# Chunked delta-rule recurrence: decays made in the setup, norms from turned rows, system in wide products, roots on GpSimd, new engine orders

## What is computed

```
q = silu(conv4(x @ Wq)); k, v = silu(conv4(x @ Wk)), silu(conv4(x @ Wv))     # 1 q, 3 k, 3 v per token and head
beta = 2 * sigmoid(x @ Wb); g = -exp(A_log) * softplus(x @ Wa + dt_bias)
q, k = l2norm(q) * d**-0.5, l2norm(k)
per token:  S = S * exp(g)
            for i in 0..2:  S = S + beta_i * k_i (v_i - k_i' S)'
            o = q' S
y = rmsnorm(o) * rms_weight * silu(x @ Wg);  out = y @ Wo
```

## Time and profile before

| what | value |
|---|---|
| median of 3 runs | 4379.42 us |
| the profiled execution's own time | 4341.66 us |
| its span, first to last instruction | 4339.9 us |
| TensorE (PE) busy | 3964.4 us, 91% |
| VectorE (DVE) busy | 3489.6 us, 80% |
| ScalarE (ACT) busy | 3345.5 us, 77% |
| GpSimd (POOL) busy | 2389.8 us, 55% |
| mean granted TensorE clock | 0.966 of 2.4 GHz |
| setup ends, recurrence ends | about 100 us, about 3482 us |

### The profile page before, as it was taken

One profiled execution on the slowest core, in us unless ns is written; L12 is line 12 of the kernel. 1 busy time (PEld: TensorE's weight loads), 2 busy tenths in 40 slices (PEclk: granted clock), 3 DMA queues, 4 the chain that ended last, 5 costly groups with the idle time before them and its releaser, 6 DMA issues. The chain is left out here.

```text
span 4339.9 us, 131624 instructions
## 1 busy us (share of the span) xinstructions
PE 3964.4 (91%) x47876; PEld 3634.2 (84%) x47876; DVE 3489.6 (80%) x9822; ACT 3345.5 (77%) x9032; POOL 2389.8 (55%) x2511
## 2 busy tenths in 40 slices
PE   1999999999999999999999999999999885999991
PEld 0799888999988888999989899999999775888881
DVE  6899999999998888999989999999999734444446
ACT  3888888888888888888888888888888722556551
POOL 3566667666766666666766666766676414000005
PEclk6999999999999999999999999999999987999995
DMA  6222333323333333223323333323333154666664
GB/s 255 66 83 87 87 87 91 87 79 84 102 87 74 82 84 89 75 83 89 100 78 85 87 85 88 92 87 83 76 104 89 45 177 141 231 226 239 232 225 130
DMA packets 307824, 485.08 MB, mean 112 GB/s; under 512 B 38784, under 2 KB 252800, under 8 KB 288384
## 3 DMA queue, kind: packets, MB, share of 16 engines
q1 hardware_dynamic: 290448, 449.65, 35.2%
q0 software_dynamic: 6144, 16.79, 1.2%
q10 hardware_dynamic: 10608, 10.23, 0.7%
HBM read 352.02 MB, written 107.75 MB: 106 GB/s over the span
## 5 line engine op out<-in xcount | busy, mean ns | idle before, releaser
L1111 DVE SCALAR_TENSOR_TENSOR conv_acc<-bank,conv_sb,conv_acc 128x256 f32<-128x256 f32 x2304 | 1089.7, 478 | 14.1 <-ACT conv_acc L922 4.7
L671 PE MATMUL bank<-x_cur,w_cur 128*128 128x259 f16 (+1 forms) x6144 | 856.7, 276 | 27.9 <-DVE v_rows L1099 24.9
L1170 DVE CAST_PREDICATED xs_lev<-mask_sb,bank 128x256 f16<-128x256 uint16 x1536 | 663.2, 432 | 98.6 <-PE bank L735 75.3
L982 ACT ACTIVATE inv<-bank 128x256 f16<-128x256 f32 x1536 | 605.4, 394 | 74.3 <-PE bank L747 51.6
L671 PEld LDWEIGHTS bank<-x_cur,w_cur 128*128 128x128 f16 (+1 forms) x6144 | 565.0, 98 | 93.1 <-DVE v_rows L1099 25.8
L1293 POOL TENSOR_TENSOR decay<-decay_tok,cst 128x512 f32<-128x512 f32 x256 | 320.0, 1273 | 489.7 <-ACT decay_tok L956 489.7
L991 ACT ACTIVATE invt<-bank 128x256 f16<-128x256 f32 x1280 | 508.3, 397 | 88.4 <-PE bank L759 72.2
L790 PE MATMUL bank<-state,kq_t 128*128 128x128 f32 x2048 | 448.3, 301 | 2.0 <-DVE state L1193 2.0
L735 PE MATMUL bank<-inv,n_high 128*128 128x64 f16 x6144 | 432.9, 193 | 3.8 <-issue 1.5
L798 PE MATMUL bank<-rhs,inv_t 128*128 128x128 f32 x2048 | 428.7, 302 | 3.1 <-DVE rhs L1186 3.1
L805 PE MATMUL bank<-w_sol,k_rows 128*128 128x128 f32 x2048 | 422.1, 298 | 2.1 <-ACT w_sol L1001 1.9
(11 more groups left out here) (245 smaller groups left out, 11482.7 us busy)
## 6 DMA issues: line engine op xcount, KB each, us to landing
w_cur<-w_parts_scratch SPq DMA_DIRECT2D x128, 1024.0 KB, 10.5
ew<-e_parts_scratch SPq DMA_DIRECT2D x117, 896.0 KB, 6.2
x_cur<-x_parts_scratch SPq DMA_DIRECT2D x128, 259.0 KB, 7.2
x_slots<-no_rows SPq DMA_DIRECT2D x128, 256.0 KB, 10.4
e_parts_scratch<-e_pair SPq DMA_DIRECT2D x96, 224.0 KB, 7.4
o_rows<-w_sol SPq DMA_DIRECT2D x512, 32.0 KB, 4.1
y_scratch<-y_buf SPq DMA_DIRECT2D x128, 128.0 KB, 10.1
y_in<-y_scratch SPq DMA_DIRECT2D x32, 512.0 KB, 4.1
```

Source lines behind the costliest of these rows:

```text
L671: last = mm(bank[i % 2][:, 0:PW], w_cur[k.i % 2][:, wp, kt, c * P:(c + 1) * P].bitcast(BF16 if wp else F16), x_cur[k.i % 2][:, xp, kt, 0:P ...
L982: a(half(inv[k.i % R_LEV][g][:], l, 0), packed(halves(LEVT), l), ACT.Copy).then_inc(t_kept.sem, 1)
L1111: v.scalar_tensor_tensor(acc, bank[at % 2][:, i:i + TB], conv_sb[:, k.h, c, i:i + 1], acc, ALU.mult, ALU.add).then_inc(tap_step.sem if i < ...
L1170: v.copy_predicated(half(xs_lev[g][l - 1][:], l, 0), half(mask4(l), l, 0).bitcast(U16), packed(halves(LEVX), l)).then_inc(x_kept.sem, 1)
```

## The change

In the setup, the decays of all blocks are made at once: VectorE multiplies (spans), TensorE sums in f32 products of 128x512, two per stretch, ScalarE takes exp and stores 512 KB per stretch to DRAM (d_dram). In the recurrence they are loaded (load_decay) instead of computed. The key scale goes into them on GpSimd (key_decay), so that system is one 128x512 VectorE operation per group. Keys are copied unscaled to k_rows by ScalarE, which squares and sums the turned rows (square_rows); the scale of the keys moves to keep_w as a scale operand. The query's norm rides in a 129th column of w_sol and o_rows. Both roots are taken on GpSimd with the power operation. norms, norms_q, decays, exp_decay, key_ln, var_ln and var_root on ScalarE are gone, and with them the table loads. The GpSimd channel's taps become one product of four windows and two additions. y_buf is a ring of 3, w_sol of 4. All six lists have a new order; stages are counted to 23, and the work lies at k[18] to k[22]. The pieces below come, in this order, from: the sizes, the setup's ScalarE, its TensorE, SyncE (load_decay and list), ScalarE, VectorE and GpSimd (powers and list).

```diff
-R_SQ = 1
+R_Y = 3
+R_CK = 3
-R_W = 3
+R_W = 4
-STAGES = 8
+STAGES = 23
...
+                    for tb in range(NTB):
+                        if tb >= 2:
+                            act.wait_ge(d_stored[tb % 2], 16 * (tb // 2))
+                        for i in range(2):
+                            act.wait_ge(spans_summed, 2 * tb + i + 1)
+                            nc.scalar.activation(decay_out[tb % 2][:, 2 * i:2 * i + 2].rearrange("p a b -> p (a b)"), bank[6 + i][:],
+                                                 ACT.Exp).then_inc(decayed, 1)
+                        act.wait_ge(decayed, 2 * tb + 2)
+                        act.dma_start(d_dram[tb], decay_out[tb % 2][:]).then_inc(d_stored[tb % 2], 16)
...
+                    for tb in range(NTB):
+                        pe.wait_ge(spans_made, tb + 1)
+                        for i in range(2):
+                            if tb:
+                                pe.wait_ge(decayed, 2 * tb - 1 + i)
+                            nc.tensor.matmul(bank[6 + i][:], cst_once[:, C_LATER_OWN],
+                                             g_upto[tb % 2][:, 2 * i:2 * i + 2].rearrange("p a b c -> p (a b c)"),
+                                             start=True, stop=True).then_inc(spans_summed, 1)
...
+                    def load_decay(k):
...
+                        at_least(sp, key_decayed, k.n - 1)
+                        sp.dma_start(decay_in[k.i % 2][:].rearrange("p a b -> p (a b)"),
+                                     bass.AP(own.tensor, own.offset, [[0, 4]] + list(own.ap))).then_inc(decay_ld[k.i % 2], 16)
...
                     def body(k):
-                        move_outputs(k[5])
-                        load(k[0])
-                        store(k[7])
-                        pieces(k[4])
+                        pieces(k[0])
+                        load_decay(k[3])
+                        store(k[9])
+                        load(k[3])
+                        move_outputs(k[7])
...
+                    def keep_k(g, k):
+                        done(act, rows_made, ("keys", g), k.n)
+                        a(k_rows[k.i % R_ROWS][:, 4 * g:4 * g + 4].rearrange("p a b -> p (a b)"), ROWS[:], ACT.Copy).then_inc(keys_kept.sem, 1)
+
+                    def square_rows(u, k):
+                        done(act, keys_kept, u // 4, k.n)
+                        a(square_out[:, u], k_rows[k.i % R_ROWS][:, u], ACT.Square, accum_out=sums[k.i % 2][:, u:u + 1])\
+                            .then_inc(squared.sem, 1)
+
+                    def keep_q(k):
+                        act.wait_ge(normed, k.n + 1)
+                        a(w_sol[k.i % R_W][96:128, :, P], k_sq[k.i % 2][96:128, :], ACT.Copy).then_inc(q_kept, 1)
...
-                        a(w_sol[k.i % R_W][:, c], chain(k), ACT.Copy).then_inc(sol_kept.sem, 1)
+                        a(w_sol[k.i % R_W][:, c, 0:P], chain(k), ACT.Copy, scale=c_k[k.i % R_CK][:, c:c + 1]).then_inc(sol_kept.sem, 1)
...
+                    def add_eps(k):
+                        done(dve, squared, 0, k.n, 1, 2, 3, 4, 5, 6, 7)
...
+                        v.tensor_scalar(k_sq[k.i % 2][:], sums[k.i % 2][:], EPS_K, None, ALU.add).then_inc(normed, 1)
...
-                        for u in range(4):
-                            last = v.scalar_tensor_tensor(n_t[g][:, u], ROWS[:, u * P:(u + 1) * P],
-                                                          c_n[k.i % 2][:, 4 * g + u:4 * g + u + 1],
-                                                          decay[:, 4 * g + u].rearrange("p a b -> p (a b)"), ALU.mult, ALU.mult)
-                        last.then_inc(rows_kept.sem, 1)
+                        v.tensor_tensor(n_t[g][:].rearrange("p a b -> p (a b)"), ROWS[:],
+                                        decay[:, 4 * g:4 * g + 4].rearrange("p u a b -> p (u a b)"), ALU.mult)\
+                            .then_inc(rows_kept.sem, 1)
...
+                    def key_root(k):
+                        pool.wait_ge(normed, k.n + 1)
...
+                        tt(sv[k.i % 2][:], k_sq[k.i % 2][:], powers[:, 0:1].broadcast_to([P, UN]), ALU.pow).then_inc(norm_made, 1)
...
+                    def var_root(k):
+                        pool.wait_ge(var_made, k.n + 1)
+                        tt(rstd[:], v_sum[:], powers[:, 1:2].broadcast_to([P, 2]), ALU.pow).then_inc(rstd_made, 1)
...
                     def body(k):
+                        minus_one(1, k[20])
+                        var_root(k[22])
+                        scale_outputs(k[22])
+                        piece(k[16])
+                        low(1, k[20])
+                        low(0, k[20])
+                        scale_windows(6, k[19])
+                        halve_taps(6, k[19])
+                        key_decay(k[19])
+                        spread_decay(0, k[19])
+                        spread_decay(1, k[19])
+                        fold_taps(6, k[19])
+                        minus_one(0, k[19])
+                        key_root(k[19])
```

More of the change, by code:

```diff
@@ L73 @@
 R_O = 2
-STAGES = 8
+STAGES = 23
 WR = 3
-MASKED = -30000.0
 EPS_K, EPS_RMS, EPS_LN = 1e-6, 1e-5, 1e-5
@@ L86, in constants @@
     before = (o[:, None] < o[None, :]) & (j[:, None] < NH)
-    neg = np.zeros((P, P), np.float32)
-    neg[:, 0:CH] = np.where((t[:, None] < np.arange(CH)[None, :]) & (j[:, None] < NH), 0.0, MASKED)
-    same = (before & (t[:, None] == t[None, :])).astype(np.float32)
     masks = []
@@ L361, in _ @@
                     gh = g_hi[:].rearrange("p n u -> p (n u)")
+                    for q in range(4):
+                        v.tensor_copy(g_heads[32 * q:32 * q + 32], g_full[0:32, 4 * q:4 * q + 4])
                     v.tensor_copy(gp[0:96], gf[0:96])
@@ L379, in _ @@
                     v.memset(tables[:, ::NTB, 2:4, 0:1], 0.0)
+                    for tb in range(2, NTB):
+                        spans(tb)
         with ExitStack() as loop_scope:
@@ L576, in halves, with free_rows @@
                 return b[:, 0:4 * HP].rearrange("p (u c) -> p u c", u=4)
+            def free_rows(eng, key, n):
+                place, reads = rows_made.places.index(key), {"keys": keys_kept}
+                slot, size = n + rows_made.order[place][1], len(rows_made.order)
+                for back in range(1, 4 * size):
+                    turn, j = divmod(place - back, size)
+                    last, stage = rows_made.order[j]
+                    if 0 <= slot + turn - stage < NIT:
+                        if last[0] in reads:
+                            done(eng, keys_kept, last[1], slot + turn - stage)
+                        else:
+                            done(eng, rows_kept, last, slot + turn - stage)
+                        return
             HP = P // 2
@@ L678, in norms @@
                     @at_stage
-                    def norms(k):
-                        pe.wait_ge(squared, k.n + 1)
-                        free(pe, rows_made, rows_kept, "norms", k.n)
-                        for u in range(UN):
-                            last = mm(ROWS[0:96, u:u + 1], squares[k.i % R_SQ][:, u].rearrange("p a b -> p (a b)"),
-                                      cst[:, C_ONES, 0:1], start=True, stop=True)
-                        last.then_inc(rows_made.sem, 1)
-                    @at_stage
                     def gram(g, k):
-                        done(pe, silu_done, 0, k.n)
-                        free(pe, rows_made, rows_kept, ("gram", g), k.n)
+                        done(pe, silu_done, 0, k.n, 1, 2, 3)
+                        free_rows(pe, ("gram", g), k.n)
                         for u in range(4):
@@ new lines, in body @@
+                        tap(5, 3, k[19])
+                        right_side(5, k[21])
+                        mask_x(5, 0, k[20])
+                        mask_x(3, 1, k[20])
+                        add_eps(k[19])
+                        invert(k[19])
+                        scale_n(k[19])
+                        new_state(5, k[21])
+                        mask_x(6, 0, k[20])
+                        right_side(6, k[21])
+                        tap(1, 1, k[18])
+                        mask_x(4, 1, k[20])
@@ L1282, in g_rows, with scale_windows @@
                     @at_stage
[L1283 to L1286 removed]
+                    def scale_windows(c, k):
+                        raw = raw_in[turn_of(c, k, ON_POOL, R_RAW)][:]
+                        windows = bass.AP(raw.tensor, raw.offset, [raw.ap[0], [1, TAPS], [1, TB]])
+                        done(pool, raw_kept, c, k.n)
+                        tt(tap_prod[:], windows, conv_sb[:, k.h, c, :, None].broadcast_to([P, TAPS, TB]), ALU.mult)\
+                            .then_inc(windows_scaled, 1)
@@ new lines, in halve_taps, with fold_taps @@
+                    @at_stage
+                    def halve_taps(c, k):
+                        pool.wait_ge(windows_scaled, k.n + 1)
+                        tt(tap_prod[:, 0:2], tap_prod[:, 0:2], tap_prod[:, 2:4], ALU.add).then_inc(taps_halved, 1)
```

(6 more changed lines are left out.)

773 lines of the change are left out of this document (356 added, 417 removed).

## The result

The changed kernel takes **4745.09 us** (median, 4727.38 to 4767.62, 4 runs), the kernel before 4379.7 beside it (4376.87 to 4382.69). The ratio is 1.084 (95% interval 1.079 to 1.088): 8.4% slower, where 4223 us, faster by 3.6%, was forecast. The profiled execution is one of 4745.15 us with a span of 4743.1. The loop that the forecast rested on is there: a train of transfers, the squares behind it, and TensorE's work up to the next train. It is longer than I made it, in both halves.

The account below looks back on a forecast made before the run. TensorE was taken to bound the kernel, at 25.73 us a block. Recurrence -182, setup +18 and fill +8 make -156 from 4341.7, and 37.8 up to the median gives 4223 us; range 4095 to 4400, chance 0.45.

Parts of the forecast that it names:

- Step 6: Output chain: transfers, squares and TensorE up to the next train form a loop of 24.3 us a block, -182 us.
- D: GpSimd's power in var_root, which TensorE waits for: at 2.5 us, 26.4 us a block, 4490 us; chance 0.12.
- Step 1: TensorE loses norms, norms_q and decays, with nothing added to its list: -1.92 us a block.
- Rival B: Clean case: the loop is loose and TensorE's list is all, 23.6 us a block, 4135 us; chance 0.20.
- Step 2: Ring of 3 for y_buf gives a store two blocks to land: -0.17 us a block on TensorE.
- Step 3: VectorE: two wide system operations at 686 ns, both keep_k gone, 20.8 us a block; counted as nothing.
- Step 4: ScalarE: table loads leave, copies and squares come, busy 22.8 becomes 23.4 us a block; counted at nothing.
- Rival C: ScalarE or the train of transfers slower: 25.3 us a block, 4350 us; chance 0.15.
- Step 5: GpSimd's new list: scale_windows 2.5 us; a power 0.4 us, between 5 ns and 2.5 us.
- Rival E: VectorE's add_eps waits for GpSimd at the shared port, 1.3 us later on average: 4388 us; chance 0.08.
- Steps 7 and 8: Setup's added f32 products, +18 us; fill ahead of the first load, +8 us; drain and fewer bodies counted 0.

Follow-up runs that it names:

- e1: The changed kernel with SyncE's move_outputs ahead of load_decay, store and load instead of behind them: 4263.17 us, ratio 0.983 to the kernel before.
- e12: The changed kernel with load_decay behind move_outputs, at the end of SyncE's body, the moves still behind the load: 4229.29 us, ratio 0.975.
- e8: The changed kernel with ScalarE's keep_res(1) ahead of square_outputs instead of behind it: 4663.23 us, ratio 1.075.
- e3: The changed kernel without the four moves and the wait for them, the outputs' rows a constant 1: 4244.07 us, ratio 0.979.
- e6: e1 with TensorE products added ahead of the turned keys, 20 of one column and two of 256, results overwritten: 4753.66 us, ratio 1.095.
- e5: e1 without ScalarE's eight square_rows, their sums a constant 64: 4258.91 us, ratio 0.981.
- e7: e1 without one of VectorE's three taps for six channels: 4252.46 us, ratio 0.980.
- e9: e1 with TensorE's turn_values(0) ahead of turn_first(0): 4262.1 us, ratio 0.982.
- e10: e9 with gram(1) ahead of fix(0), solve(0) behind level_x(5,1) and level_tt(4,1), and ScalarE's keep_tt(4,1) ahead of keep_w(0): 4383.54 us, ratio 1.011.
- e11: e1 with the ring of y_buf back at 2: 4258.38 us, ratio 0.982.
- e4: The changed kernel with both powers on GpSimd replaced by multiplications, so no roots are taken: 4709.51 us, ratio 1.085.

## Why the prediction was wrong, point by point

*Step 6, the output chain, is the step that failed*, in both halves of its sum, not in there being a loop. The sum was a train of 11.9, work of 2.0 and TensorE's 10.2, 24.1 in all.

- **The train of 11.9 measured 13.7 to 14.7 (median 13.8).** The issue of the four moves was taken from before at 2.57 and took 4.41 (median 4.43), and a landing at 4.1 took 5.5 (median; 5.9 for the last of the four, the one that is waited for). The distance from the train's start to the first move was shorter, 4.3, than the 5.9 that is left of 11.9, and hid a part of this. Before, the first move stood 6.73 us behind the load; here it stands 2.7 behind, right behind x_cur and w_cur, 1.3 MB. I shortened the train by issues and kept the durations that the longer distance had given. e1 (1.9 us a landing) and e12 (2.6 at 6.8 us distance) show that they go with what is in the queue.
- **The remainder of 12.2 measured 15.3 (mean 15.0).** Two terms were too small. The work from the squares to turn_outputs was 2.0 and took 3.1 in the mean: I closed it through sum_squares, the power and the scaling, but turn_outputs was never waited for. TensorE was already stopped ahead of it, at level_tt(1, 0), the 32nd entry of its list (turn_outputs is the 36th), by keep_res(1) right behind the squares in ScalarE's list, and with that out of the way by VectorE's tap behind sum_squares (e8). The text had named the "46 entries queued behind" and did not price them. And TensorE's stretch from turn_outputs to the next body's start was 12.0 and took 13.5. In e12, at a clock of 1.00 and with hardly a pause (the wait at L802 is 6.6 us in the whole window), the same two distances are 2.6 and 13.0. So most of the second miss is no matter of the pause: the 13.1 that I had counted by entries was right, and taking it down to 12.0 for the short level products was wrong. From the squares to the end of the body the changed kernel takes 1.1 us more than e12. That is about the most that the lowered clock behind the pause (0.57 for four microseconds in the block shown) can have cost there; the forecast had nothing for it.

29.0 for 24.1: at 28.55 - 25.73 = +2.8 a block the recurrence lost 358 us where I had -182. "Slower" had a chance of 0.16, nearly all of it by way of the power (D, 4490 us). The kernel came out slower still, by a way that had no chance of its own.

The trace of before had the price of a small transfer close behind the load. There SyncE stored y_buf two issues behind w_cur; its tile shows the store's issue (min/median/max, ns) and its landing:

```profile
L613 SPq DMA_DIRECT2D y_scratch<-y_buf x128: 320/3142/4095, 254.7 to 3482.1; - x128
...
DMA to landing us min/median/max: 1.7/10.1/12.6
```

In the changed kernel the same store goes out ahead of the load, and takes 0.43 us to issue and 3.8 to land (medians). The change moved the moves into the place that the store had had.

*Step 1* was right in its amount (1.93 by starts, 1.92 forecast) and wrong in what it was worth. Even with the moves out of the way, e1, e3 and e12 stand at 24.9 to 25.2, and 1.2 to 1.4 of the 1.9 came back, a third of it as idle time and the rest as longer steps of the products that stayed. Added work costs 1 to 1 (e6), relief of one of the others brings nothing (e5, e7). Rival B's 23.6 is not reached even without the moves (e3, 25.03). I took TensorE's list as 25.73 less what was removed, as if the new order had the steps of the old one. Why these steps grew is open: e9 and e10 show only that two of the waits can't be taken out one by one.

*Step 2*: nobody waits for y_buf's store after the change, as forecast; on top of e1 the third buffer is worth 0 (e11), not 0.17.

*Step 3*: the two wide systems take 684 ns each, as the nearest row (686) said. But VectorE is busy for 1788.25/79.0 = 22.6 us a block in e1, not 20.8.

*Step 4*: a square is 314 ns plus 205 for its sum, a keep_w 366 where I allowed at most 473. ScalarE in e1 is busy for 1803.0/79.0 = 22.8 us a block, below the 23.4 forecast. There is one table load in the recurrence, in its first block. Rival C was headed "ScalarE or the train slower": the train was slower, but only ScalarE's part of it had been priced, and that did not come to be.

*Step 5*: var_root takes 695 ns, not 400, and key_root 1650; both inside my bounds of 0 and 2.5, and neither matters (e4). scale_windows takes 1898 ns for 1024 columns, not 2500: its cost per column falls from the 1273 for 512.

*Rival E*: add_eps takes 649 ns in the mean, below the 1 us that I set as its sign. But what E describes does happen, at a smaller price. In each of the 69 blocks of the window add_eps starts beside GpSimd's halve_taps (L1310) and ends some 0.03 us after it; in the 11 blocks of e1 in which GpSimd stands still it takes 163 ns. One of the two products `first` (L1175) fares alike beside minus_one, at 0.77 us instead of 0.28. From VectorE's, GpSimd's and TensorE's order of time in e1:

```profile
2022.92 1.27 POOL L1350 TENSOR_TENSOR n_t<-n_t,cst 128x512 f32<-128x512 f32 x1 [0.19 <-DVE n_t L1167]
2023.57 0.77 DVE L1175 TENSOR_TENSOR first<-n_high,mask_sb 128x256 f16<-128x256 f16 x1
2024.39 0.40 PE L772 MATMUL bank<-ident,first 128*128 128x128 f16 x4 [0.33 <-DVE first L1175]
```

Each is 0.5 us, not the 1.3 of rival E. The delay of add_eps stands ahead of key_decay, and so ahead of the train in the changed kernel; that of `first` is the wait of TensorE that e9 went after. No run took GpSimd's operations from beside them.

*Steps 7 and 8*: SyncE's first issue in the recurrence is at 114.80 (forecast 115 to 122), and TensorE's first product at 133.73, 23.2 later than in the earlier trace rows, where 18 + 8 = 26 were forecast. Yet the first output is 1.1 us earlier than before: from TensorE's first product to it are 79.1 us instead of 103.4. I had put a block's fewer bodies against the other effects of the fill and counted 0; 24.3 came of it.

## What to carry to other kernels

A queue's durations belong to its order. When transfers move closer together, an issue or a landing taken from the old trace is no longer its price: ask what stands in front of the small transfer in its queue, and how long ago that was issued. And a wait at the head of an in-order list shifts everything behind it; the cheapest repair here was one line moved to the end of SyncE's body, which turned 8.4% slower into 2.5% faster. Where an engine's work is cut and its order is made anew, compare the steps that remain as well as the sum, for TensorE gave back 1.2 to 1.4 of 1.9 us here. Where an operation changes places with another behind a large transfer, look up what the other one paid there: the old trace had it.

## What the runs showed that was not expected

- In this kernel a small transfer right behind a large one is slow twice over: the issue of four moves takes 4.41 us instead of 2.55, and each lands after 5.5 us instead of 1.9 (changed kernel against e1). The longest single issue in the changed kernel's window is 3.87 us, in e1's 1.91.
- Many of TensorE's pauses are followed by some microseconds at or near the lower clock, as in the block shown, where six products take 1.16 us instead of 0.83. It is not each of them: of 71 pauses of 0.9 us or more in the window, 46 have a granted clock below 0.7 over the 4 us behind them and 25 have 1.00. With the pauses nearly gone (e1), the window's clock is 0.99. The Trainium skill (TensorE: Matmul & The Clock Gate, HAM oscillation — how this bites in real kernels) describes a kernel in which a wait for a DMA lets the clock fall anew at every tile. This trace agrees for the pauses with a low clock behind them, such as the one of 3.87 us with 0.57, and not for the 25 others.
- A VectorE operation of 8 columns can stand until a GpSimd operation beside it ends: 649 ns instead of 163 (add_eps; rival E above).
- GpSimd's power costs 695 ns for 2 columns and 1650 for 8, which is far more than its 1273 ns for 512 columns of other arithmetic would give; the same two as multiplications take 195 and 208 ns (e4).
